# ScalarE rounds a gated batch's transposes ahead of the next batch's norm, in place of behind it

## The reference, cut to what matters

```python
amp = sigmoid(x @ amp_w + amp_b); ph = tanh(x @ ph_w + ph_b) * pi
h = (cos(ph) + sin(ph)) * amp
for l in range(2):
    e = h @ ent_w[l] + ent_b[l]
    ent = e @ ent_pw[l] + ent_pb[l]
    h = layer_norm(h + ent, ln3_g[l], ln3_b[l])
    t = einsum('bsd,pdf->pbsf', h, path_w[l]) + path_b[l]
    h = layer_norm(h + sum(t * (cos(phase[l]) + sin(phase[l]))), ln4_g[l], ln4_b[l])
x = layernorm(x + h)
```

## Time and profile before

| | |
|---|---|
| median of 3 runs | 1081.36 us (1079.01 to 1081.61) |
| the profiled execution, its own time | 1078.66 us |
| its span in the trace | 1076.9 us |
| PE, DVE, ACT, POOL busy | 1008.6, 748.3, 611.3, 373.6 us |
| mean granted clock of TensorE | 0.976 of full |

### The profile page before, as it was taken

One profiled execution on the slowest core, in us unless ns is written; L12 is line 12 of the kernel. 1 busy time (PEld: TensorE's weight loads), 2 busy tenths in 40 slices (PEclk: granted clock), 3 DMA queues, 4 the chain that ended last, 5 costly groups with the idle time before them and its releaser, 6 DMA issues.

```text
span 1076.9 us, 18320 instructions
## 1 busy us (share of the span) xinstructions
PE 1008.6 (94%) x6633; PEld 839.2 (78%) x6633; DVE 748.3 (69%) x2042; ACT 611.3 (57%) x1177; POOL 373.6 (35%) x725
## 2 busy tenths in 40 slices
PE   6989999999998887989999999999999999999995
PEld 5555555555667786777899999999999999999995
DVE  5666777867639668867657767766776775677746
ACT  5566567664368565745645666554666645566640
POOL 4454364562131464353822222322222332222600
PEclk9899989998999899999999999999999999999998
DMA  7000000022110001022201010110101001010111
GB/s 245 21 2 21 3 22 21 22 61 79 59 46 4 1 2 40 1 98 60 79 1 40 1 40 1 40 40 1 40 1 40 3 38 40 1 40 1 43 37 40
DMA packets 29234, 36.91 MB, mean 34 GB/s; under 512 B 1780, under 2 KB 26584, under 8 KB 29144
## 3 DMA queue, kind: packets, MB, share of 16 engines
q1 hardware_dynamic: 24872, 31.28, 9.1%
q10 hardware_dynamic: 4272, 4.46, 1.3%
HBM read 31.40 MB, written 4.20 MB: 33 GB/s over the span
## 4 chain that ended last, share of the span: by engine, by line
PE 54%; DVE 5%; ACT 1%; issue 1%; POOL 1%; DMA 1%; SPq 0%; DVEq 0%; POOLq 0%
PE ps L1886 24%; PE ps L1869 24%; PE ps L1759 2%; PE ps L1841 2%; PE ps L1810 1%; DMA mlp_b<-L_ffn_LN_B 1%; DVE ln_stats L86 1%; DVE ln_stats L2244 0%; ACT x_b L2029 0%; DVE att L2327 0%; PE ps L1801 0%; DVE xT_l L2286 0%; DVE xT_l L2262 0%; DVE rsum L2343 0%; DVE amp L2270 0%
## 5 line engine op out<-in xcount | busy, mean ns | idle before, releaser
L2107 ACT ACTIVATE G<-ps,bias_col 128x512 f32<-128x512 f32 x192 | 135.5, 706 | 186.3 <-PE ps L1869 176.8
L1886 PE MATMUL ps<-w_h,G_h 128*128 128x256 f32 x736 | 208.2, 283 | 0.0
L1886 PE MATMUL ps<-w_h,G_l 128*128 128x256 f32 x736 | 207.9, 282 | 0.0
L1886 PE MATMUL ps<-w_l,G_h 128*128 128x256 f32 x736 | 207.8, 282 | 0.0
L2375 DVE TENSOR_TENSOR G_l<-G,G_h 128x512 fp32r<-128x512 f32 x192 | 155.1, 815 | 60.0 <-ACT G_h L2108 60.0
L1688 POOL TENSOR_TENSOR x_a<-xn,mlp_g 128x1024 f32<-128x1024 f32 x20 | 67.6, 3379 | 344.8 <-DVE xn L2405 344.8
L693 ACT ACTIVATE probs<-ps 128x512 f32<-128x512 f32 (+3 forms) x256 | 98.3, 440 | 107.5 <-PE ps L833 107.4
L1869 PE MATMUL ps<-xT_h,w_h 128*128 128x512 f32 x384 | 152.0, 396 | 1.1 <-issue 1.1
L1869 PE MATMUL ps<-xT_h,w_l 128*128 128x512 f32 x384 | 150.6, 392 | 0.0
L1869 PE MATMUL ps<-xT_l,w_h 128*128 128x512 f32 x384 | 150.3, 392 | 0.0
L1102 DVE CUSTOM_DVE_ANT_0 ps<-ps,q_mask 128x128 f32<-128x128 f32 (+3 forms) x256 | 120.7, 512 | 36.3 <-PE ps L822 34.8
(11 more groups left out here) (303 smaller groups left out, 2128.4 us busy)
## 6 DMA issues: line engine op xcount, KB each, us to landing
w_raw<-L_ffn_W_T SPq DMA_DIRECT2D x12, 1024.0 KB, 5.2
hs<-L_attn_hidden_states SPq DMA_DIRECT2D x8, 512.0 KB, 4.0
x_kept<-hs SPq DMA_DIRECT2D x4, 512.0 KB, 3.4
w_raw<-x_kept SPq DMA_DIRECT2D x2, 1024.0 KB, 5.5
out<-xn SPq DMA_DIRECT2D x3, 512.0 KB, 2.9
w_raw<-L_ffn_ent_w_T SPq DMA_DIRECT2D x1, 1024.0 KB, 10.8
w_raw<-L_ffn_ent_pw SPq DMA_DIRECT2D x1, 1024.0 KB, 12.7
heads_T<-neg_rows SPq DMA_DIRECT2D x64, 2.0 KB
```

Source lines behind the costliest of these rows:

```text
L1886: mm = pe.matmul(ps[:, 4 + t // 2, (t % 2) * D:(t % 2 + 1) * D], x[b % 2][f][:, t * P:(t + 1) * P], w2_chunk(w, f), start=(k == 0), stop=( ...
L2107: act.activation(G32[n % 4], bank, ACT.Gelu, bias=bias)
```

## The change

Before, ScalarE has normalise(0), the rounding of the gated batch 3, normalise(1), and then high(k), normalise(k+2) for k = 0 to 11: a batch is rounded behind the norm of the batch after it. Now it has normalise(0), the same rounding, and then high(k), normalise(k+1): each batch is rounded ahead of that norm. At the last k the order stays normalise(12), high(11), normalise(13).

```diff
         normalise(0, 0)
         gated_high(act, g, 3)
-        normalise(0, 1)
         for st in range(END):
 
             for b in range(B):
-                high(st, b)
-                normalise(*divmod(st * B + b + 2, B))
+                if (st, b) == (END - 1, B - 1):
+                    normalise(END, 0)
+                    high(st, b)
+                    normalise(END, 1)
+                else:
+                    high(st, b)
+                    normalise(*divmod(st * B + b + 1, B))
                 if st == 1:
                     attention_weight_high(b)
```

## The result

The changed kernel takes 1071.53 us (median of 8 runs, 1067.27 to 1073.61), against 1078.60 us before (median of 8, 1075.26 to 1081.61). The ratio is 0.9927, with a 95% interval of 0.9909 to 0.9944: 7.9 us less by the ratio (6.0 to 9.8), 7.1 by the medians. The eight runs of before lie lower than the three that I had, whose median was 1081.36. The forecast was 1074.0, from the median of those three and a gain of 6.6.

A forecast was written before the change was run, and what follows sets the result against it. TensorE, busy 94%, bounds the kernel except where it waits in a loop through ScalarE, VectorE and GpSimd. A gain of 6.6 gives 1078.66 - 6.6 = 1072.1, or 1074.8 from the median; forecast 1074.0 us, range 1070.0 to 1078.2.

The forecast's parts named there:

- The loop: Old order in the wave: normalise, high, low, moments, root, normalise takes 9.58 us for two steps, 10.39 with weights.
- The hand-over: turn(k) to turn(k+1) through ScalarE's high and norm: 3.7 us, hidden by linear on TensorE below 4.18 a step.
- The long way round: Three-step path from turn(k) through linear, moments, root and norm: 12.3 us, 4.1 a step, just under 4.18.
- The sum: Step times added along the wave: turn(9) at 398.00, low(10) at 406.20, all behind it 6.6 us earlier.
- GpSimd's step beside a weight: In the wave, where a weight's remainder is made beside GpSimd's root, GpSimd bounds at 4.30 us a step.
- the 4.6 that I had named as a sign of being wrong: Turns in the wave standing above 4.6 us apart would show the forecast wrong; 4.2 to 4.3 was expected.
- The range's bound of 1.8 us a root: Each GpSimd root beside a weight pays 1.8 us more, the step is 5.8, the gain only 3.6 us.
- The start: Wave's first turns: high(1) is late, normalise(2) slips some 0.2 us, linear(4) hides that; turn(2) stays at 368.58.
- The wave's end: low(10) starts at 406.20, not 412.81; low(11), the attention's sum and all behind move by the same 6.6 us.
- first rival: GpSimd's steps pay more, or the attention doesn't move: gain mostly given back, 1078 to 1081 us; chance 0.12.
- The clock (second): TensorE's clock fall near the attention's start may land elsewhere: up to 3.3 us either way, 1071 to 1078; no separate chance.
- The slower rival: normalise(k+1) waits for turn(k); 1.6 us more per step makes it 3.2 us slower, 1084 or more; chance 0.04.

The follow-up runs named there:

- first_half: New order up to k = 5 and the old one from k = 6, against the kernel before: 1074.32 us, ratio 0.9971.
- second_half: Old order up to k = 5 and the new one from k = 6, against the kernel before: 1076.15 us, ratio 0.9979.
- pad4: Changed kernel plus four unread activations (1.82 us) ahead of each of normalise(1) to normalise(11): 1084.90 us, ratio to before 1.0066.
- spread: Changed kernel with attention weights rounded behind every second norm, remainders behind moments(5), (7), (9), (11): 1069.92 us, ratio to before 0.9929.
- last_high_first: Changed kernel with the last exception removed, so high(11), normalise(12), normalise(13): 1073.85 us in one run.

## Why the prediction was right, and where it was off

**The loop.** Right. The old order's 9.58 us for two steps, 10.39 with weights, gave way to TensorE's floor: turn(3) at 373.88 is 4.18 behind turn(2), as forecast, and the steps stay 4.17 to 4.18 up to turn(7). first_half and second_half show that both halves of the wave make the gain.

**The hand-over.** Right: 3.7 us, shown by pad4. The long way round came out too: turn(2) 369.70, moments(5) 374.08 (4.38; forecast 4.39), and root(5) to normalise(5) 3.94 (forecast 3.95).

**The sum.** Forecast 398.00 - 368.58 = 29.42 us from turn(2) to turn(9), measured 30.05. The term that was mis-sized is GpSimd's step beside a weight: I took 4.30 from a trace in which GpSimd had idle time ahead of each root, so that a remainder could only meet a root's first step. With the roots back to back, a remainder can meet the last steps of a root as well. root(8) paid twice, 0.29 us on its first step and 0.48 on its last, and root(9) paid 0.46 on its last but one, where I had 0.29 for each root. So turn(7) to turn(8) took 4.73 us and turn(8) to turn(9) 4.45. Together that cost 0.6 us, and spread gets it back. The 4.73 is above the 4.6 that I had named as a sign of being wrong; it was so at this one step only. In all turn(2) to low(11) fell by 6.02 us; I had 6.6. That the measured time lies 2.5 us under the forecast is mostly the base: the three runs that I started from had a median 2.8 us above that of the eight. The range's bound of 1.8 us a root was far from what happened.

**The start.** Here the sum had nothing, and turn(2) "stays". That was true only with the clock at 1.2 GHz over turn(1), as in the profile that I read: there the gain is 55.35 - 49.2 = 6.1 us, an estimate as the 49.2 is. At 2.4 GHz it is 55.32 - 47.76 = 7.6 us. The 7.9 us of the runs (6.0 to 9.8) hold both.

**The wave's end.** Right, low(10) as the place from which all moves: low(10) to low(11), and low(11) to the load of the blocks' constants, are what they were in the pair before and after. The exception at the last k carries 1.2 us, as last_high_first shows.

**The rivals.** GpSimd did become the bound of some steps (first rival), but at 4.4 to 4.7 us, not 5.8. The clock (second) moved the place of its fall from one profile to the next. In the pair before and after, low(11) to the end of the trace is 1076.9 - 418.13 = 658.8 us and 1071.9 - 413.23 = 658.7, so there the clock made no difference. In the pair profiled again it is 1080.4 - 420.64 = 659.8 and 1071.1 - 413.84 = 657.3: 2.5 us that go with the place of the fall and come on top of the wave's 7.6. The earlier place is also that of two kernels which keep half of the old order, so the new order isn't needed for it; whether it makes it more frequent was not tested. The slower rival came true only with pad4's 1.8 us. I had put 1.6 us at each hand-over as what makes the kernel 3.2 us slower; the straight line above puts that at about 1.7, and no gain at 1.3.

**The port.** The rule that the prediction took from "SBUF — State Buffer", "Who interferes with whom", of the Trainium skill (a VectorE operation contends with a GpSimd one that reads SBUF if it has two SBUF inputs, and not with one) held for which operations disturb GpSimd: in the changed kernel low falls on running roots throughout, and from root(2) to root(11) none without a weight beside it took more than 3.98 us to its norm. The charge was below the operation's full length, 0.28 to 0.50 us for a `tensor_tensor` of 0.66: a step that was hit ended 0.05 to 0.09 us after the operation, and its own 0.2 us is not charged.

## What to carry to other kernels

In an engine that works strictly in order, ask of each instruction with a long wait what stands behind it and was ready already; here 1.1 us of ready work stood behind a wait for another engine, and TensorE, which bounds the kernel, waited nine times for what hung on it. When such an order is turned round, add up the loop that it closes (here 3.7 us) and compare it with what hides it (4.18), and leave the order as it is where somebody waits for the instruction that would be put last. And when a stretch speeds up, price the neighbours at the new spacing: idle time ahead of each root had kept a collision to its first step, at 0.29 us; without it one root met two, and a hit cost up to 0.5.

## What was not expected of the hardware

Two VectorE operations of two SBUF tensors in a row held up two GpSimd steps in a row by about 0.5 and 0.3 us, and not one step for the whole 1.2 us. And the clock over one turn decided what the change was worth inside the wave, 6.1 us (an estimate) or 7.6: the old order took 55.3 us from turn(1) to low(11) at either level, the new one about 49.2 (the estimate) and 47.8. One profile of before, at one of the two levels, didn't show that.
